# LoRA products of a quantised layer on 64-row halves of TensorE, issued in alternating pairs

## What is computed

```
x = x + (x @ W0.T + b0 + coeff * (x @ sign(mask)))                 # layer 0, per batch a 1024x1024 mask
delta = lora_B @ lora_A * 0.5                                       # [1024,64] @ [64,1024]
wg    = (weight + delta) / scale                                    # scale per row and group of 128 columns
w_q   = cb[searchsorted(thresholds, wg)] * scale                    # codebook of 8 levels
x = x + x @ (w_q + delta).T                                         # layer 1
x = x + x @ W2.T + b2 + 2 * (x @ A2[id]) @ B2[id]                   # layer 2, rank 16
x = x + (x @ B3[id].T) @ A3[id].T                                   # layer 3, rank 16
```

## Time and profile before

| | us |
|---|---|
| median of 3 runs | 550.1 |
| range of the runs | 549.83 to 550.27 |
| the profiled execution, its own time | 549.03 |
| its span, first to last instruction | 547.4 |

### The profile page before, as it was taken

The page is one execution under the profiler, slowest core; times in us unless marked ns, Lnnn a source line. Parts: engine busy times, 40 slices in busy tenths (PEclk is TensorE's granted clock), DMA queues, the critical chain, the costliest instruction groups (busy, mean ns, idle before and its releaser), DMA issues.

```text
span 547.4 us, 9005 instructions
## 1 busy us (share of the span) xinstructions
PE 531.3 (97%) x2864; PEld 458.2 (84%) x2864; DVE 461.2 (84%) x742; ACT 350.7 (64%) x681; POOL 169.0 (31%) x170
## 2 busy tenths in 40 slices
PE   4899999999999999999999999999999999999997
PEld 4898788888888788888888888888888888888886
DVE  5997898988865879987999889897897987989853
ACT  3776775776745774675767657666676665766730
POOL 2669767987734320003004003000300400400120
PEclk9999999999999999999999999999999999999999
DMA  8767031833395993458446455746845645564222
GB/s 228 247 86 152 24 117 43 255 128 125 89 208 167 356 333 61 151 185 173 131 141 188 92 179 168 124 151 193 160 135 152 175 101 182 169 108 154 77 50 77
DMA packets 147281, 82.57 MB, mean 151 GB/s; under 512 B 105060, under 2 KB 124516, under 8 KB 147124
## 3 DMA queue, kind: packets, MB, share of 16 engines
q1 hardware_dynamic: 145444, 78.34, 52.1%
q0 software_dynamic: 1520, 3.86, 2.7%
q10 hardware_dynamic: 288, 0.01, 0.0%
HBM read 65.93 MB, written 16.26 MB: 150 GB/s over the span
## 4 chain that ended last, share of the span: by engine, by line
PE 75%; DVE 11%; DMA 4%; ACT 4%; SPq 3%; issue 2%; DVEq 0%; ACTq 0%
PE bank L1679 17%; PE bank L1686 9%; PE bank L1723 5%; PE bank L1722 5%; PE bank L1553 5%; PE bank L1721 5%; PE bank L1555 5%; PE bank L1554 5%; PE bank L1772 3%; PE bank L1770 3%; PE bank L1771 3%; DVE merged_ring L1207 3%; PE bank L1734 2%; DVE m_lo L1213 2%; PE bank L1463 2%; DMA mask_ring<-in_mask_Bx4096x_ik 2%
## 5 line engine op out<-in xcount | busy, mean ns | idle before, releaser
L1679 PE MATMUL bank<-x_t_pair,m_hi 128*128 128x512 f32 x512 | 128.8, 394 | 1.9 <-ACT m_hi L820 1.7
L605 POOL TENSOR_TENSOR x_t_pair<-x_sum,x_t_pair 128x256 fp32r<-128x256 f32 x32 | 29.8, 959 | 290.9 <-ACT x_t_pair L893 290.9
L1679 PEld LDWEIGHTS bank<-x_t_pair,m_hi 128*128 128x128 f32 x512 | 92.6, 189 | 19.9 <-ACT m_hi L820 3.1
L820 ACT CAST m_hi<-merged_ring 128x512 fp32r<-128x512 f32 x128 | 73.0, 619 | 51.0 <-PE bank L1686 25.7
L810 ACT ACTIVATE merged_ring<-mask_ring,batch_now 128x1024 f32<-128x1024 int32 x64 | 78.1, 1243 | 25.1 <-DMA mask_ring<-in_mask_Bx4096x_ik 24.3
L1213 DVE TENSOR_TENSOR m_lo<-merged_ring,m_hi 128x512 fp32r<-128x512 f32 x128 | 84.6, 709 | 9.1 <-ACT m_hi L820 9.0
L1207 DVE TENSOR_TENSOR merged_ring<-merged_ring,w_t 128x1024 f32<-128x1024 f32 x64 | 76.4, 1221 | 14.3 <-ACT merged_ring L810 13.3
L1686 PEld LDWEIGHTS bank<-x_t_pair,m_lo 128*128 128x128 f32 x512 | 69.9, 191 | 5.0
L1686 PE MATMUL bank<-x_t_pair,m_lo 128*128 128x256 f32 x512 | 71.5, 283 | 0.0
L1723 PE MATMUL bank<-P_hi,x_t_pair 128*128 128x496 f32 x160 | 61.5, 385 | 0.0
L1722 PE MATMUL bank<-P_lo,x_t_pair 128*128 128x496 f32 x160 | 61.5, 384 | 0.0
(11 more groups left out here) (221 smaller groups left out, 1110.2 us busy)
## 6 DMA issues: line engine op xcount, KB each, us to landing
mask_ring<-in_mask_Bx4096x_ik SPq DMA_DIRECT2D x64, 512.0 KB, 4.4
w_nat<-in_L_cond_W SPq DMA_DIRECT2D x14, 512.0 KB, 5.1
x_t_squares<-in_x SPq DMA_DIRECT2D x56, 128.0 KB, 3.0
w_raw<-in_L_cond_weight SPq DMA_DIRECT2D x16, 256.0 KB, 4.8
out<-out_staged SPq DMA_DIRECT2D x16, 248.0 KB, 5.5
w0t_dram<-w_out SPq DMA_DIRECT2D x14, 256.0 KB, 2.7
w_t<-w0t_dram SPq DMA_DIRECT2D x6, 512.0 KB, 5.0
g_batch<-g_dram POOLq DMA_DIRECT2D x21, 128.0 KB, 4.2
```

Of the source, the lines that this page charges most:

```text
L820: nc.scalar.copy(Mh[:, n % MR], ring_f[:, k % MR, h * HALF:(h + 1) * HALF]).then_inc(s["h_set"], 1)
L1679: mm(bank[L0_BANK[HT * h + j]][:, :], Mh[:, n % MR, j * P:(j + 1) * P], xThl[:, :, :, k + i, :], start=(k + i == 0), stop=False, skip_grou ...
```

## The change

The 64 rows of lora_B and lora_A stand twice, in rows 0 to 63 and 64 to 127. `lb_nat` holds the rows of both output halves side by side, so four transposes of 128 columns give `lora_b_t` with half 0 in the lower and half 1 in the upper rows; one ACT scaling copies it. Loading takes two transfers more (lora_B in two pieces, lora_A again behind the scales). A product now reads 64 rows: the lower ones for half 0, the upper ones for half 1, and the eight products of a slice are issued alternately as `delta_pair(q)`, at one place instead of two.

Both halves need a bank at once. The even halves always use bank 3, the odd ones banks 4 and 5 in turn. So that bank 3 comes free, ACT copies it to SBUF as `delta_kept` (L663 of the new file) once add_delta has read it, and effective(2q) reads the copy, for q = 0 to 6. Pair q waits for that copy of slice q-1.

```
-        def dps(n):
-            return bank[3 + n % 3]
+            return bank[4 + n // 2 % 2 if n % 2 else 3]
-        DELTA_STEPS = {0: (2, 6), 1: (2, 5)}
+        DELTA_STEPS = {0: 2, 1: 2}
...
-            sp.dma_start(lbn[:, :, :], lora_b.rearrange("(t p) r -> p t r", p=P)).then_inc(s["lora_b_in"], 16)
+            for h in range(2):
+                sp.dma_start(lbn[:, :, h], lora_b.rearrange("(h t p) r -> h p t r", h=2, p=P)[h]).then_inc(s["lora_b_in"], 16)
...
+            sp.dma_start(la[RL:2 * RL, :], lora_a).then_inc(s["lora_a_in"], 16)
...
             sp.wait_ge(s["delta_done"], 2 * G)
+            sp.wait_ge(s["eff_set"], 2 * G - 3)
             load_x(0)
...
+            def delta_copy(q):
+                act.wait_ge(s["raw_used"], 2 * q + 1)
+                if q:
+                    act.wait_ge(s["eff_set"], 2 * q - 1)
+                nc.scalar.copy(dkept[:, :], dps(2 * q)[:, :]).then_inc(s["delta_kept"], 1)
...
                 if n + 1 < 2 * G:
                     norm(n + 1)
+                if n % 2 == 0 and n < 2 * G - 2:
+                    delta_copy(n // 2)
                 if n % 2 == 0 and n > 4:
                     p_hi((n - 4) // 2, range(1, 2))
...
-            nc.vector.memset(la[RL:P, :], 0.0).then_inc(s["lora_pad"], 1)
-            nc.vector.memset(lbt[RL:P, :], 0.0).then_inc(s["lora_pad"], 1)
...
-                ins = nc.vector.tensor_tensor(acc[:, h], pooled[:, h], dps(n)[:, :], ALU.add)
+                kept = h == 0 and q < G - 1
+                if kept:
+                    dve.wait_ge(s["delta_kept"], q + 1)
+                ins = nc.vector.tensor_tensor(acc[:, h], pooled[:, h], dkept[:, :] if kept else dps(n)[:, :], ALU.add)
...
+            def delta_half(n, t):
+                q, rows = n // 2, slice(n % 2 * RL, (n % 2 + 1) * RL)
+                return mm(dps(n)[:, t * P:(t + 1) * P], lbt[rows, t * P:(t + 1) * P], la[rows, q * P:(q + 1) * P],
+                          start=(t == 0), stop=True, skip_group_check=True)
+
+            def delta_pair(q):
+                if q == 0:
+                    pe.wait_ge(s["lbt_set"], 1)
+                else:
+                    pe.wait_ge(s["delta_kept"], q)
+                if q >= 2:
+                    pe.wait_ge(s["eff_set"], 2 * q - 2)
                 for t in range(HT):
+                    for h in range(2):
+                        ins = delta_half(2 * q + h, t)
+                        if t == HT - 1:
+                            ins.then_inc(s["delta_done"], 1)
...
-                    if t in DELTA_STEPS.get(g, (0, 5)):
-                        m = 2 * g + 4 + t // HT
-                        if m < 2 * G:
-                            delta(m)
+                    if t == DELTA_STEPS.get(g, 0) and g + 2 < G:
+                        delta_pair(g + 2)
```

More of the change, by code:

```diff
@@ L107, in cond_resid_chain @@
     a2n = at("a2_nat", [P, KT, NB, R], F32, lo + 4 * KB)
-    lbn = at("lb_nat", [P, KT, RL], F32, lo + 28 * KB)
+    lbn = at("lb_nat", [P, HT, 2, RL], F32, lo + 28 * KB)
     own = at("own_batch", [P, NB, R], F32, reg_z3 + 20 * KB)
@@ L167, in cond_resid_chain @@
     c_sum = at("c_sum", [P, HW], F32, reg_la + 2 * KB)
-    lbt = at("lora_b_t", [P, D], F32, reg_b2)
+    lbt = at("lora_b_t", [P, HALF], F32, reg_b2)
+    dkept = at("delta_kept", [P, HALF], F32, reg_b2 + 2 * KB)
     off = [reg_c]
@@ L222, in cond_resid_chain @@
             s_set v_set h_set m_ready m_used l0_done x1_part x1_sum x1_hi x1_ready0 x1_ready1 x_turned xt_hi xt_first xt_later xt_ready u_done u_part u_summed u_hi u_ready
-            out_done out_added out_st0 out_st1 out_st2 out_st3 c_in gl_in c_stored lora_pad now_set coef_now
+            out_done out_added out_st0 out_st1 out_st2 out_st3 c_in gl_in c_stored delta_kept now_set coef_now
             t_step t_summed t_hi t_ready a_summed a_hi a_ready prod_done c_sums c11_set out_copied b2_split side_set side_done side_step side_st""".split()}
@@ L718, in b2_set @@
                     nc.scalar.copy(b2h[:, :], b2r[:, :]).then_inc(s["b2_split"], 1)
-            for h in range(2):
-                act.wait_ge(s["lbt_tr"], h + 1)
-                nc.scalar.mul(lbt[0:RL, h * 512:(h + 1) * 512], bank[5 + h][0:RL, :], L1_SCALE).then_inc(s["lbt_set"], 1)
+            act.wait_ge(s["lbt_tr"], 1)
+            nc.scalar.mul(lbt[:, :], bank[5][:, :], L1_SCALE).then_inc(s["lbt_set"], 1)
             act.wait_ge(s["sc_in"], 16)
@@ L732, in _ @@
             mid_up(0)
+            delta_copy(0)
             w2_hi(2)
@@ L747, in _ @@
             w1_hi(1)
+            delta_copy(1)
             mid_up(2)
@@ L1445, in _ @@
             pe.wait_ge(s["ident_set"], 1)
-            pe.wait_ge(s["lora_b_in"], 16)
-            for h in range(2):
-                for t in range(HT):
[L1450 to L1455, removed]
-                    pe.wait_ge(s["eff_set"], n - 2)
-                elif n == 0:
-                    pe.wait_ge(s["lbt_set"], 2)
-                for t in range(HT):
-                    k = h * HT + t
-                    ins = mm(dps(n)[:, t * P:(t + 1) * P], lbt[:, k * P:(k + 1) * P], la[:, q * P:(q + 1) * P],
-                             start=(t == 0), stop=True, skip_group_check=True)
-                ins.then_inc(s["delta_done"], 1)
+            pe.wait_ge(s["lora_b_in"], 32)
+            for t in range(HT):
+                ins = nc.tensor.transpose(bank[5][:, t * P:(t + 1) * P], lbn[:, t].rearrange("p h r -> p (h r)"), ident[:, :])
+            ins.then_inc(s["lbt_tr"], 1)
+            def delta_half(n, t):
[9 more added lines that the diff above has]
+                    pe.wait_ge(s["eff_set"], 2 * q - 2)
+                for t in range(HT):
+                    for h in range(2):
+                        ins = delta_half(2 * q + h, t)
+                        if t == HT - 1:
+                            ins.then_inc(s["delta_done"], 1)
             def w0_transpose(blk, h):
@@ L1478, in w0_transpose @@
                 ins.then_inc(s["w0_tr"], 1)
-            pe.wait_ge(s["lora_pad"], 2)
-            pe.wait_ge(s["lora_a_in"], 16)
-            delta(0)
-            delta(1)
+            pe.wait_ge(s["lora_a_in"], 32)
+            delta_pair(0)
             def w2_transpose(t):
@@ L1538, in _ @@
             v_part(4)
-            delta(2)
+            delta_pair(1)
             w2_transpose(5)
@@ L1545, in _ @@
             v_part(7)
-            delta(3)
             COLS = [(0, 512), (512, 1024), (1024, EXT)]
```

## The result

The changed kernel takes **553.44 us** in the median (553.21 to 553.84, 6 runs), the kernel before 550.18 on the same chip (6 runs). The ratio is 1.0062, interval 1.0049 to 1.0076: slower by 3.3 us, where 549.6 was forecast and 552.6 was the upper end. The profiled execution took 553.21 us with a span of 551.5, so 1.7 lies around it; it is 4.2 us above the profiled execution before (549.03).

What follows compares the result with a forecast made beforehand. PE and the DVE/ACT chain close the stage together; the later ledger counts. DVE/ACT: +0.5 start, +0.5 and +0.3 port, +0.1 copies, -0.95 twice, giving -0.5 us from 550.1, so 549.6 us; range 547.2 to 552.6.

Steps and rivals of the forecast that it cites:

- the port: DVE's effective(2q) adds, now with both inputs in SBUF, wait for POOL: +0.5 us at effective(2), +0.3 for halves 9 to 13.
- start: Kernel start: SP's two extra transfers delay the codebook and raw weights; +0.5 us, bounds 0 and +1.1.
- copies: Seven ACT copies between norm and the second P_hi cast, partly offset by PE's lead: +0.1 us in all.
- halves 12 and 14: With PE early, the DVE/ACT step from terms_c to the next half shortens by 0.95 us in each.
- Pairs: PE's LoRA products: two halves overlap, 0.89 us plus at most 0.15 instead of 1.78; pairs 3 to 7 save 4.45.
- Rival A: No overlap on PE: each pair keeps 1.78 us, delaying gsum(1) by 1.3 us in group 2; 552.4 us, chance 0.26.
- Two ledgers: Up to the stage's end, PE (-2.9 us) and DVE/ACT (-0.5 us) are summed separately; only the later one counts.
- the prediction's signs: Expected if the forecast is right: among others, PE idle before group 7, which starts about 0.5 us earlier than 161.85.
- Rival B: PE's ledger rules the stage because DVE's chain has more give: -2.9 us, 547.2 us, chance 0.10.
- Beyond the stage the shift passes on: After the stage, the shift carries through, since PE's own progress releases SP's first w_t load at 169.13 us.
- Rival C: Copies and ports cost in full on the DVE ledger, effective(6) and effective(8) losing 0.7 us each; 551.1 us, chance 0.20.

Runs made afterwards that it cites:

- Run one: Changed kernel with effective(2q) reading its delta from a PSUM bank again, the ACT copies still running unread: 549.66 us, ratio 0.9995 to the kernel before.
- run nine: Kernel before with only the operand changed: effective(0, 2, ... 12) reads 512 columns of the lora_a tile in SBUF: 553.64 us, ratio 1.0070.
- runs ten and eleven: POOL's 64 sums cut to 32 of 512 columns, in the changed kernel (550.84 us) and in the kernel before (551.40 us).
- Run four: Changed kernel with the SBUF read of effective(2q) kept only for slices 4 to 6, PSUM reads for slices 0 to 3: 550.53 us, ratio 1.0004.
- run seven: As run two, but four products per slice instead of eight, both halves reading the even half's delta: 550.44 us, ratio 1.0010.
- run two: Changed kernel with PSUM reads for effective(2q) and without the seven ACT copies, pairs waiting for the raw add: 549.23 us, ratio 0.9987.
- run six: As run two, but with the transfers of the kernel before and the upper rows of lora_A zeroed: 549.63 us, ratio 0.9985.
- run five: Changed kernel with 10 and 8 filler identity transposes on PE at the start: 553.61 us.
- run three: Changed kernel with four lower-row products issued ahead of the four upper-row ones, not alternating: 555.56 us.

## Why the prediction was wrong

**The step that failed is the port, by its size.** The prediction named it with its mechanism, and priced seven adds at +0.8 us in all (0.5 for effective(2), 0.3 for effective(8) to (12) together, nothing for effective(0), (4) and (6)). Run one measures 3.8 us, run nine 3.7 (553.64 - 549.97) without any of the rest, and runs ten and eleven show that POOL is the other party. So 3.0 of the 3.8 us between forecast (-0.5) and result (+3.3) are this term; the rest is about what start, copies and halves 12 and 14 miss together, 0.2 to 0.3 each. Three readings were wrong in it.
- *How often.* Five of the seven adds are long, and their excess is 4.7 us. POOL was read as busy 25 of 30 us, but a share says less than the order: effective(n) runs while POOL sums the terms that DVE has just written for the next half, so the collision is built in.
- *The follower.* The identity add behind it collides again, 1.24 to 1.27 us in slices 1 to 3. The 0.90 us maximum of the earlier trace rows was there to see, but no second wait was added to the first. In run nine it is this add, late, for which PE waits 1.93 us at 54.44, in place of 0.57 before.
- *Where it is exposed.* Of the early adds only effective(2) was held to be on a chain. Run four puts 2.9 of the 3.8 us on slices 0 to 3, and the starts of terms_c in the changed kernel, less those in run one, say where: -0.45 us in half 0, 0.2 in halves 1 to 3, 1.8 in 4 and 5, 2.15 in 6 and 7, 2.5 in 8 and 9, 3.1 from 10 on. So effective(2) costs 1.56 us where 0.5 were put down. The step at effective(0) is 0.64 us, with the start's scatter in it, and 0.38 each at (4) and (6), for nothing put down; effective(8) costs 0.55. The waits that were to absorb the rest do so in part: the 0.78 us for norm takes up effective(10) and (12), which cost nothing, and the wait ahead of gsum 1.3 of the 1.7 us that effective(6) and its follower lose.

The Trainium skill, page "SBUF — State Buffer", section "Who interferes with whom", gives the rule: a DVE instruction with two SBUF inputs and a GpSimd instruction that reads SBUF exclude each other. By that rule, runs nine and ten agree, at 1.52 us in the median with POOL and 0.68 without.

**Pairs: overlap right, price too low.** The halves run side by side, and run seven shows the overlap complete; but a pair costs PE 1.28 us where 0.89 and at most 0.15 more were forecast. The extra was read on one side only, from the step behind a half, in a trace without products on 64 rows. The saving is 0.50 a pair, not 0.89. Rival A (no overlap) is out, though its pair of about 1.1 us was reached: by its sum the ga products would cost gsum(1) 0.44 us (2 x 0.39 - 0.34), and in run two gsum(1) is 0.64 us late (88.04 against 87.40) behind a start that is 0.76 late. The Trainium skill, page "TensorEngine Tiling (Array Packing)", section "Key Properties", has tiles work in parallel and a change of mode drain the engine. On the first the trace agrees (1.09 us for sixteen alternated and for eight alone). The second fits the 0.39 us that a group on 64 rows costs more, but that a drain is its cause no run here shows.

**Start: size right, cause not shown.** The first terms_c stands at 20.90 us against 20.16, 0.74 late for a forecast of 0.5, but run six has it at 21.41 with the old transfers. It stands at 20.16 to 20.27 in the three kernels with the old products and at 20.65 to 21.41 in all the others. In the changed kernel DVE waits 0.24 and 0.16 us for w_hi at 14.71 and 15.56, behind the first w2 transposes, which begin at 12.94 (12.48 before) and take 1.97 us (1.21). Whether the late tile or the half pace does it stays open; run five did not remove either.

**Copies: 0.4 us** of the median by run two (0.1 forecast), not distinguished from zero. They do show in PE's waits, 0.98 us ahead of the pair of group 1.

**Halves 12 and 14: right in kind.** 0.72 us in half 12 for 0.95 forecast; over the two the lag shrank by 1.66 (5.07 to 3.41) for 1.9.

**Two ledgers: the tie held, the rest is not shown.** Group 7 starts 0.84 us behind the last P_lo in this kernel and in run two. But PE was not idle before it, as the prediction's signs wanted (starts at 165.12 and 165.26), and 0.55 us more of PE for each pair moved the last P_lo by 2.95 us in run three. So PE's time counts when it grows; that a saving counts for nothing was tested by no run, since run seven saves PE nothing. Rival B's 547.2 is out by its price: with 0.50 in place of 0.89 a pair its -2.9 becomes about -0.95, and run two, without copies and slow reads, is 0.9 us below its own before, not clear of the noise.

**"Beyond the stage the shift passes on": right for a loss, wrong for a gain.** 3.41 us of lag arrived in a profiled execution that is 4.2 longer; a lead of 1.3 us was waited away by 188.75 us for a mask tile. This did not cause the miss. If the mask tile lands at that time whatever comes ahead, as in the traces of before and of runs two and seven, a gain of the stage is lost for the most part.

**Rival C** had the right mechanism, "copies and ports cost in full", and its sign that a gsum comes later than 88 us appeared (91.66). Its price of +1.5 on the ledger still took two late adds at 0.7, where five adds were long by 0.8 to 1.3 each and three followers by 0.4 to 0.9 (1.25 us against 0.36 to 0.90 in run one). Its sum is also off as written: two adds at 0.7, 0.6 for the start and 0.5 for half 3 make +2.5, or 552.1 us, not +1.5; that too is under the measured time.

## What to carry to other kernels

Before an operand of a DVE add moves from PSUM to SBUF, look at what POOL runs in those microseconds, not at its share: where POOL works through what DVE wrote a moment ago, such an add often pays the rest of a POOL instruction (five of seven here), and the next one pays again. Price a group of products from the last instruction ahead of it to the second one behind it, not from its own starts: here that turned a saving of 0.69 us into 0.50. The overlap saved PE 0.50 us a pair and no run could tell its gain from nothing; the operand that moved cost 3.8 us. A gain at the end of a stage counts only up to the next transfer that is waited for whatever the stage did; look for that wait before costing the stage.

## What the runs showed of the hardware

- A DVE add of 128x512 float32 with both inputs in SBUF takes 0.68 us alone and mostly 1.46 to 2.09 us beside POOL's work; with one input in PSUM, 0.68 or 0.69 in all 16 cases of run one, POOL as busy as ever (168.1 us against 169.2).
- The exclusion costs POOL as well: a sum of 1.29 us took 1.52 to 1.56 us behind a delayed add, and 1.86 us where DVE came first.
- Products on 64 rows overlapped when upper and lower rows alternated: sixteen instructions in 1.09 us, grouped by half 1.64, on 128 rows 1.78. With the steps around them: 1.28, 1.83, 1.78.
- Eight on the lower rows alone take the same 1.09 us as sixteen alternated. Against eight on 128 rows (0.89 with the steps around them) a group on 64 rows costs 0.39 us more.
- A product's own duration hardly differs (272 ns alternated, 276 before); only the distance of the starts tells the cases apart.
